# Merged attention weights computed inside the blocks ahead of them

## The reference

```python
def _L3_attn_ref ...
    k_eff = (W_dq.T @ W_uq.T @ W_uk).reshape(nh, hs, kvl)
    v_eff = (W_uv.T @ W_o.T).reshape(kvl, nh, hs).transpose(1, 0, 2)
    c_kv = x @ W_dkv.T
    q = (x @ W_dq.T @ W_uq.T).reshape(B, T, nh, hs).transpose(0, 2, 1, 3)
    q_lat = jnp.einsum('bhtd,hdl->bhtl', q, k_eff)
...
def _attention(x, Wq, Wkva, Wkvb, Wo):      # in _L3_ffn_ref
    q = (x @ Wq).reshape(b, t, H, D).transpose(0, 2, 1, 3)
    ckv = x @ Wkva
    kv_latent, k_rope = (ckv[:, :, :R], ckv[:, :, R:])
    kv = (kv_latent @ Wkvb).reshape(b, t, H, NOPE).transpose(0, 2, 1, 3)
...
    return y @ Wo
```

## Time and profile before

| | |
|---|---|
| median of 3 runs | 1993.07 us (1988.14 to 1995.74) |
| profiled execution, first to last instruction | 1991.5 us |
| instructions | 34855 |
| PE busy | 1615.1 us (81%) |
| DVE busy | 1231.2 us (62%) |
| ACT busy | 823.4 us (41%) |
| POOL busy | 606.1 us (30%) |
| mean granted TensorE clock | 0.892 of full speed |

### The profile page before, as it was taken

The page is one execution under the profiler, slowest core; times in us unless marked ns, Lnnn a source line. Parts: engine busy times, 40 slices in busy tenths (PEclk is TensorE's granted clock), DMA queues, the critical chain, the costliest instruction groups (busy, mean ns, idle before and its releaser), DMA issues. The chain is left out here.

```text
span 1991.5 us, 34855 instructions
## 1 busy us (share of the span) xinstructions
PE 1615.1 (81%) x12400; PEld 1077.5 (54%) x12400; DVE 1231.2 (62%) x4249; ACT 823.4 (41%) x1760; POOL 606.1 (30%) x742
## 2 busy tenths in 40 slices
PE   3378767888779897757988799978877888999888
PEld 1146434454547787644444366745546654677556
DVE  6868645575378999533666333326848875899632
ACT  2232345366227786732344443314643410333422
POOL 4605122430024535304531000022202115777221
PEclk8677877999879999878999898889988987999999
DMA  2000001320036777613321000022210000000000
GB/s 86 0 12 1 10 30 50 83 60 14 7 128 213 262 248 262 219 37 116 84 58 38 18 1 0 1 61 65 62 61 3 1 0 1 2 2 3 2 0 22
DMA packets 81332, 115.59 MB, mean 58 GB/s; under 512 B 8464, under 2 KB 62608, under 8 KB 80400
## 3 DMA queue, kind: packets, MB, share of 16 engines
q0 software_dynamic: 18432, 67.38, 9.7%
q1 hardware_dynamic: 60144, 44.90, 8.1%
q10 hardware_dynamic: 2592, 1.18, 0.3%
HBM read 88.85 MB, written 1.05 MB: 45 GB/s over the span
## 5 line engine op out<-in xcount | busy, mean ns | idle before, releaser
L2643 POOL DMA_INDIRECT f_rows<-tree_table,f_index x128 | 128.8, 1006 | 185.8 <-DVE f_index L2704 75.7
L2844 PE MATMUL f_ps_y<-f_rows,shared_sb 128*128 128x128 f32 x1024 | 129.2, 289 | 31.3 <-ACT f_rows L2916 31.3
L2916 ACT ACTIVATE f_rows<-f_rows,f_low_act 128x128 f32<-128x128 f32 x512 | 153.0, 387 | 0.8
L1667 ACT ACTIVATE x_probs<-x_ps_z 128x768 f32<-128x768 f32 (+1 forms) x128 | 117.4, 917 | 85.6 <-PE x_ps_z L1527 57.6
L82 POOL TENSOR_TENSOR rstd<-moments,shared_sb 128x12 f32<-128x12 f32 (+3 forms) x22 | 4.6, 207 | 480.9 <-DVE moments L66 480.8
L2844 PEld LDWEIGHTS f_ps_y<-f_rows,shared_sb 128*128 128x128 f32 x1024 | 124.5, 203 | 37.2 <-ACT f_rows L2916 33.9
L2743 DVE CUSTOM_DVE_ANT_0 f_rows<-f_rows,f_xn 128x128 f32<-128x128 f32 x512 | 111.3, 287 | 24.2 <-DMA f_rows<-tree_table,f_index 24.2
L1357 DVE TENSOR_REDUCE x_minus_max<-x_ps_s 128x4 f32<-128x1024 f32 x64 | 77.8, 1223 | 73.7 <-PE x_ps_s L1527 73.5
L2095 PE MATMUL f_ps_h<-f_xnT,weights 128*128 128x512 f32 x144 | 76.7, 661 | 2.4 <-ACT f_hT L2160 2.1
L2160 ACT ACTIVATE f_hT<-f_ps_h,weights 128x512 f32<-128x512 f32 x72 | 48.6, 685 | 71.4 <-PE f_ps_h L2095 69.7
L2072 DVE SCALAR_TENSOR_TENSOR x_tokens<-f_ps_y,f_chosen,x_tokens 128x128 f32 (+1 forms) x128 | 36.0, 344 | 67.1 <-PE f_ps_y L2107 67.1
(11 more groups left out here) (661 smaller groups left out, 4191.6 us busy)
## 6 DMA issues: line engine op xcount, KB each, us to landing
x_queries<-x_pieces SPq DMA_DIRECT2D x96, 64.0 KB, 2.1
x_keys<-x_pieces SPq DMA_DIRECT2D x84, 64.0 KB, 2.1
a_queries<-a_pieces SPq DMA_DIRECT2D x48, 64.0 KB, 2.1
weights<-w_L_ffn SPq DMA_DIRECT2D x1, 2953.5 KB, 9.9
a_keys<-a_pieces SPq DMA_DIRECT2D x42, 64.0 KB, 2.1
weights<-w_L_ffn SPq DMA_DIRECT2D x1, 2449.0 KB, 9.7
weights<-w_L_ffn SPq DMA_DIRECT2D x1, 2176.0 KB, 9.2
f_rows<-tree_table,f_index POOLq DMA_INDIRECT x128, 6.1
```

Source lines behind the costliest of these rows:

```text
L1667: a.activation(probs[:, r % HELD, :, :], ps_z[:, :, 0:WIDE], ACT.Exp, scale=scale).then_inc(exped, 1)
L2643: pool.indirect_dma_start(rows[:, place(u, j), tree, :], None, g.tree_table, bass.IndirectOffsetOnAxis(index[:, u % 2, low, j * TREES + tr ...
L2844: last = pe.matmul(ps_y[:, u % SUMS, j, :], g.ident, rows[:, place(u, j), tree, OUT + f * D:OUT + (f + 1) * D], start=False, stop=(low, j, ...
L2916: last = a.activation(row, row, ACT.Copy, scale=low_act[:, u % 3, j * TREES + tree, f:f + 1])
```

## The change

Two pieces of weight arithmetic move into the blocks ahead of the ones that use them.

1. The block with the latent attention's products goes. The seven products are issued by PE in the last turn of the experts, at e = 5, 6 and 7, between `up(e)` and `down(e - 1)`; the six copies by DVE after the additions of items 4, 5 and 6. The results lie in three tiles that now live for the whole program, the products in two further PSUM banks (the experts' block then uses all eight). The six semaphores move along, and so does their clearing, by SP, from one block to the next.
2. The rotary attention's eight product steps go from the start of `layer3_rotary` into slots 18 to 21 of `layer3_block`, in place of the 5 fillers of these slots: one group of line 3190 and one product of line 3197 in each, into the score bank that the MLP slots no longer use. DVE clears and copies its part in slot 18, after `add_mlp(17)`, and copies the products in slot 22. The 16 fillers and eight waits between the products go.

```diff
 def layer3_latent_attention(nc, g, w):
-        with ExitStack() as psums, nc.Block() as block:
...
+    weights = dict(w, **{n: m[:, :] for n, m in zip("qkv", g.latent_w)})
...
@@ layer2_experts, vector, turn @@
                     last.then_inc(added, 1)
+                    if is_last and e >= MERGED_AT - 1:
+                        take_merged(e)
...
+            def take_merged(e):
+                if e == MERGED_AT - 1:
+                    v.wait_ge(first_made, 1)
+                    v.tensor_copy(g.latent_w[0][:, :], ps_w[:, 0, 0:P])
+                    v.tensor_copy(wide[:, :], ps_w[:, 0, P:2 * P])
+                    v.tensor_copy(values[:, :], ps_w[0:32, 1, 0:P]).then_inc(first_ready, 1)
+                elif e == MERGED_AT:
+                    v.wait_ge(second_made, 1)
+                    v.tensor_copy(narrow[:, :], ps_w[0:32, 1, P:2 * P]).then_inc(second_ready, 1)
+                elif e == MERGED_AT + 1:
+                    v.wait_ge(third_made, 1)
+                    v.tensor_copy(g.latent_w[1][:, :], ps_w[:, 0, 0:P])
+                    v.tensor_copy(g.latent_w[2][:, :], ps_w[:, 0, P:2 * P]).then_inc(third_ready, 1)
+                    v.wait_ge(third_ready, 1)
...
@@ layer2_experts, tensor, turn @@
                             up(t, CH * e + c)
+                    if is_last and e >= MERGED_AT:
+                        merge(e)
...
+            def merge(e):
+                if e == MERGED_AT:
+                    pe.wait_ge(g.loaded["L3_attn"], 16)
+                    pe.matmul(ps_w[:, 0, 0:P], latent["dq"], latent["uqT"], start=True, stop=True)
+                    pe.matmul(ps_w[:, 0, P:2 * P], latent["uqT_plain"], latent["dq_wide"], start=True, stop=True)
+                    pe.matmul(ps_w[0:32, 1, 0:P], latent["uv"], latent["oT"], start=True, stop=True).then_inc(first_made, 1)
+                elif e == MERGED_AT + 1:
+                    pe.wait_ge(first_ready, 1)
+                    pe.matmul(ps_w[0:32, 1, P:2 * P], latent["uk"], wide[:, :], start=True, stop=True).then_inc(second_made, 1)
+                elif e == MERGED_AT + 2:
+                    pe.wait_ge(second_ready, 1)
+                    pe.matmul(ps_w[:, 0, 0:P], latent["dkv"], narrow[:, :], start=True, stop=True)
+                    pe.matmul(ps_w[:, 0, P:2 * P], latent["dkv"], values[:, :], start=True, stop=True).then_inc(third_made, 1)
...
@@ layer3_block, vector, end of a slot @@
+                if slot == MERGED_FROM:
+                    v.wait_ge(g.loaded["L3_ffn"], 16)
+                    v.memset(g.rotary_q[:, :, LATENTS:PLAIN], 0.0)
+                    v.tensor_copy(g.rotary_q[:, :, PLAIN:HEAD],
+                                  rotary["q"].rearrange("p (h d) -> p h d", h=HEADS)[:, :, PLAIN:HEAD])
+                if slot == MERGED_FROM + 4:
+                    v.wait_ge(parts_made, 8)
+                    v.tensor_copy(g.rotary_q[:, :, 0:LATENTS],
...
+                    v.tensor_copy(g.rotary_vo[:, :, :],
...
+                        .then_inc(parts_taken, 1)
+                    v.wait_ge(parts_taken, 1)
...
@@ layer3_block, tensor @@
+            def merge(j):
+                if j == 0:
+                    pe.wait_ge(g.loaded["L3_ffn"], 16)
+                    pe.wait_ge(max_ready, 2 * UNITS)
+                else:
+                    pe.wait_ge(parts_made, 2 * j)
+                for c in range(HEADS // 4):
...
+                last.then_inc(parts_made, 1)
...
...
-                fill_wait(pe, g, ps_c[:, :], 512, 5 if mlp_at(slot) is not None else 2)
+                if MERGED_FROM <= slot < MERGED_FROM + 4:
+                    merge(slot - MERGED_FROM)
+                else:
+                    fill_wait(pe, g, ps_c[:, :], 512, 5 if mlp_at(slot) is not None else 2)
...
@@ layer3_rotary, tensor @@
             pe.wait_ge(g.loaded["L3_ffn"], 16)
-            for j in range(4):
...
-                last.then_inc(w_made, 1)
-                fill_wait(pe, g, ps_s[:, 0, :], 512, 2)
-                pe.wait_ge(w_made, j + 1)
-            for c in range(4):
...
-                fill_wait(pe, g, ps_s[:, 0, :], 512, 2)
-                pe.wait_ge(w_made, 4 + c + 1)
             pe.wait_ge(const_ready, 1)
```

More of the change, by code:

```diff
@@ L2212, in layer3_block @@
                              "steps", "pool_steps", "const_ready"))
+        parts_made, parts_taken = sem("parts_made"), sem("parts_taken")
+        rotary = g.weights["L3_ffn"]
+        PLAIN, LATENTS, HEADS, HEAD = 32, 16, 16, 64
+        MERGED_FROM = ITEMS.index((MLP, 0)) + 2
         block = ctx.enter_context(nc.Block())
@@ L2481, in down @@
                 last.then_inc(y_made, 1)
+            def merge(j):
+                plain, both = (ps_s[:, i, :, :].rearrange("p j k -> p (j k)") for i in range(2))
+                rows = slice(PLAIN * j, PLAIN * (j + 1))
+                if j == 0:
[4 more added lines that the diff above has]
+                for c in range(HEADS // 4):
+                    h = 4 * c + j
+                    last = pe.matmul(plain[:, h * LATENTS:(h + 1) * LATENTS], rotary["q_plainT"][rows, c * P:(c + 1) * P],
+                                     rotary["kvbT"][rows, c * LATENTS:(c + 1) * LATENTS], start=True, stop=True)
+                last.then_inc(parts_made, 1)
+                rows = slice(HEAD * (j % 2), HEAD * (j % 2 + 1))
+                pe.matmul(both[rows, j // 2 * D:(j // 2 + 1) * D], rotary["kvb_blocks"][:, j * HEAD:(j + 1) * HEAD],
+                          rotary["o"][:, j * P:(j + 1) * P], start=True, stop=True).then_inc(parts_made, 1)
             transpose(0)
@@ L3079, in _ @@
             v.tensor_copy(halves16[:, :], w["halves"]).then_inc(const_ready, 1)
-            v.memset(w_q[:, :, LATENTS:PLAIN], 0.0)
-            v.tensor_copy(w_q[:, :, PLAIN:HD], w["q"].rearrange("p (h d) -> p h d", h=NH)[:, :, PLAIN:HD])
             def take_factor(part, of):
```

66 lines of the change are left out of this document (16 added, 50 removed).

## The result

| | before | changed |
|---|---|---|
| median of 5 runs each, taken together | 1988.52 us (1988.14 to 1995.74) | 1979.83 us (1976.32 to 1980.47) |
| ratio to before | | 0.9935, 95% interval 0.9917 to 0.9953 |
| span of the profiled execution | 1991.5 us | 1974.9 us |

The forecast was 1979.7 us. The medians lie 8.7 us apart, the means 12.1 us (1990.8 and 1978.7). Before's runs fall in two heaps, at 1988 and at 1993 to 1996, and the two medians caught different sides of them; by the ratio the gain is 0.65%, 12.9 us. The 13.4 us of the forecast are to be held against these, and not 1979.83 against 1979.7.

The account below looks back on a forecast made before the run. No engine bounds the whole kernel; two seams between blocks are on the path. Gains of 3.4 and 13.1 less 0.7 and 2.4 make 13.4 us, so 1993.07 becomes 1979.7 us; the stated range is 1973.5 to 1988.

Parts of the forecast that it names:

- The seam of the latent attention: Between experts and latent attention: the latent products' block goes, 5.8 us gained, nothing behind it becomes late.
- Products among the experts: Experts' last turn: 14 product records at 0.146 us cost 2.0 us, plus a 0.35 us PE wait at e = 6.
- Part 1: Latent products moved into the experts' last turn: 5.8 - 2.0 - 0.35 = 3.4 us gained (1.4 to 4.1).
- Rotary start: Start of the rotary attention: ACT's first copy 13.65 us earlier, 0.5 lost to the late clock rise; 13.1 us gained.
- 3 x 0.24: MLP slots 19 to 21: products busy 2.58 us against the fillers' 2.34 at 1.2 GHz; 0.7 us lost.
- 2 x 1.21: MLP slots 22 and 23: the clock stays down, 6.31 us each instead of 5.10; 2.4 us lost.
- A third term: MLP slot 18: DVE's memset and copy, 0.6 us, come at the slot's end and cost nothing.
- The cover of 0.95 us: MLP slots: DVE idles 0.95 us for POOL, which hides its memset and copies; without that cover 1.5 us.
- The first rival: MLP slots: the clock returns in slot 21 or 22 as before, giving 2.4 us back; 1977.3 us, chance 0.25.
- The cold start: Rotary attention: clock at 1.2 GHz from fillers to first scores; 6.5 us gained, 1986.6 us, chance 0.12.
- dip: Experts' last turn: clock falls to 0.50; 10 us long gives 1984.7 us, chance 0.10; without end 1998.0, chance 0.04.
- The first tokens: Rotary attention: its first tokens would wait for something else, so almost no gain; 1992.8 us, chance 0.04.

Follow-up runs that it names:

- early: Changed kernel with DVE's first three copies of the latent products ahead of item 4's additions instead of behind them; 1974.31 us (one run).
- twice: Changed kernel with each of the six latent products issued twice into the same place; 1980.70 us (one run).
- part1: Kernel before with only the latent products moved into the experts' last turn, rotary products left in place; 1986.97 us, ratio to before 0.9982.
- both: The changed kernel run once more, unaltered, against the kernel before on the same chip; 1976.95 us, ratio to before 0.9937.
- part2: Kernel before with only the rotary products moved into the MLP slots, latent products keeping their block; 1983.09 us, ratio to before 0.9967.
- slot17: Changed kernel with the rotary products one slot earlier, in slots 17 to 20; 1976.09 us, ratio to before 0.9928.
- best: Changed kernel with five fillers kept behind the products, as in fills, and the copies moved, as in early; 1973.12 us, ratio to before 0.9908.
- fills: Changed kernel with the five fillers kept behind the rotary products in slots 18 to 21; 1972.76 us (one run).
- nofill: Changed kernel without the fillers (3 a slot) ahead of the rotary attention's first slot of scores; 1978.49 us, ratio to before 0.9928.
- gap: part1 with the five fillers of slots 18 to 21 taken out and nothing put in their place; 1988.80 us, ratio to before 0.9981.
- hot: Changed kernel with 10 fillers in slots 16 to 18, 3 behind the products in slots 19 to 21, 8 in 22 and 23; 1985.50 us (one run).
- fills5: Five further runs of the same kernel as fills, against the kernel before; 1974.16 us, ratio to before 0.9904.

## Why the prediction was right

That the median meets the forecast to 0.1 us is luck. The forecast stands on 1993.07, the median of three runs of the kernel before; five runs put it at 1988.52. What was right is the gain: 13.4 us forecast, 12.5 in the profiled pair and 12.9 by the ratio, with errors inside its terms that in part cancel.

**The seam of the latent attention: right.** 5.8 us worked out, 5.81 measured, and nothing became late behind it: the latent attention's first scores come 24.4 us after the block's start, where they came after 24.8. SP's further clearing cost nothing that the trace shows.

**Products among the experts: the sum right by luck.** 2.0 for the records and 0.35 for the wait were 2.35; measured 2.4. But the 2.0 is 14 x 0.146, and there are six products and 12 records, which give 1.75 and a sum of 2.1. `early` puts the wait at 0.15, `twice` the 12 records at 1.66; what was left out is the other 0.6, about 0.3 us for each of the two groups that stand alone. The two records too many and the wait that was too long made up for it. Part 1 comes to 5.8 - 2.4 = 3.4 us, as worked out; part 1 alone measured 3.6.

**Rotary start: right within 0.4 us.** 13.65 us to ACT's copy, measured 13.56. The clock rose later than estimated: at 0.50 up to 1652.6, 4.6 us behind the first filler and not 4, so the chain behind the copy took 0.8 us more, not 0.5. This term is not one number: the chain takes 6.9 to 7.0 us in `both`, `part2`, `slot17`, `early` and `best`, where the clock is up by the time of ACT's copy, 7.5 in `fills` and 7.7 here, where it comes 1.0 and 1.4 us behind it, and 8.2 in `twice`, at 2.4 us. That the step is sized rightly doesn't show that the fillers help: `nofill` is as fast up to the first scores without them.

**The MLP slots: 3.6 us where 3.1 were worked out, and both terms mis-sized.** The term "3 x 0.24" came from busy times, 2.58 against 2.34. Measured, a slot at 1.2 GHz with products takes 6.91 us against 6.31, so 0.6 more. By their starts, from the first filler to the next `down` it is 2.14 us (1623.71 to 1625.85), from the group to the next `down` 2.44 (1609.93 to 1612.37), and the transpose ahead and the first step of `down` behind take 0.3 more together. The weight load of that `down` starts 0.43 us ahead of it behind the fillers, and with it behind the products (the row at 1612.36). The kernel before:

```profile
1625.42 0.76 PEld L2479 LDWEIGHTS x_ps_z<-weights,x_hT 128*128 128x128 f32 x2 [0.28 <-issue]
1625.85 0.64 PE L2479 MATMUL x_ps_z<-weights,x_hT 128*128 128x128 f32 x2
```

The cost shows in the intervals of slots 20, 21 and 22, so 1.8 instead of 0.7. In slot 19 it is nothing: the 6.31 us of the prediction are one interval, that of slot 21; before the change slot 19 took 5.10 and slot 20 5.67. The term "2 x 1.21" was too large: the low stretch lasted one slot longer and not two (27.3 us against 17.1, less what lies in slot 18), and it ended in the fillers of slot 22; 1.2, and 0.3 more where the fall comes earlier in its slot. A third term was put at nothing and cost 0.33: in slot 18 DVE's memset and copy of 128x512 stand beside POOL's first step of the reciprocal deviation, which takes 0.52 us there and 0.20 elsewhere, and DVE's layer norm waits for POOL. It takes 0.52 in all eleven kernels that have the two instructions there and 0.20 in the three that don't (before, `part1`, `gap`); which of the two does it was not separated. The cover of 0.95 us that the prediction named was a wait for just the instruction that they slow. The Trainium skill, "SBUF — State Buffer", "Who interferes with whom", says that VectorE and GpSimd share one port pair with an exclusive lock, which VectorE's copies can take in their two-port modes; the row agrees in direction, with 0.3 us, and can't say who held the pair.

**The clock.** That the products would not bring it up was right: 25.78 of 26.00 us busy at 0.50 in the changed kernel, 30.20 of 30.20 in `part2`. The reason given was thinner than it had to be: it spoke of the products, but in `gap` the clock stays down 23.9 us without them, and `fills` shows that they do no harm where the fillers stay. The Trainium skill, "TensorE: Matmul & The Clock Gate", Part 1, has sustained activity release the clock. By a simple reading of that rule, busy is enough; these stretches with a fully busy PE at 1.2 GHz speak against it. The first rival, the clock that returns in slot 21 or 22, came half: it returned in slot 22, in the fillers that stand there again, but so late that this slot took 6.90 us; slot 23, which the forecast had at the low clock as well, took 5.10.

**The other rivals.** The cold start came in its mechanism, 5 us at 0.50, but at the price of 0.8 us; cold all through and without the fillers (`nofill`) the start costs nothing up to the first scores. A start that is cold all through with the fillers in place was not seen; the dearest was `twice`, with 1.3 us. No dip came in the experts: in the changed kernel it stands at 1.00 from 1296 to 1309.6, and `twice`, with double the products, has no low stretch there either. The first tokens waited for nothing else.

Taken together 3.4 + 12.75 - 3.6 = 12.55 us against the forecast's 13.4.

## What to carry to other kernels

Small weight products belong into a dense TensorE stream of an earlier part: they cost 0.11 to 0.16 us a record and about 0.3 us a group, where a block of their own costs the whole chain of handovers. But where they take the place of fillers, keep the fillers behind them and look at the granted clock: the products alone kept the engine busy for 26 us and more without bringing it back, and with the fillers kept it was low for 7 us in three traces of three. It is no rule: five fillers a slot without products left it low for 17. Price a replaced piece by intervals of the slot at the clock that will hold there, not by busy times, and look which other engine the covered copy slows.

## What the runs showed of the hardware

- TensorE can be busy without a pause for 30 us and stay at 1.2 GHz (`part2`, 30.20 of 30.20 us: f32 products with 128 and 256 columns, one-row bias products, 16-column products, and in the last two slots five fillers each); in another kernel it fell from 2.4 GHz while busy 5.00 of every 5.00 us (`hot`). With five fillers of 128x512 bf16 behind the products of each slot it was back after 3.4 us, twice (`fills`); with as many and no products it stayed low for 17.1 us (before).
- An f32 group of eight records with 16 columns takes 1.06 us at 2.4 GHz and 1.89 at 1.2 (line 2514).
- A low clock need not cost anything: without fillers and products the MLP part took 40.1 us with 23.9 us at 0.50, and 41.9 us before the change with 17.1.
- A VectorE memset of 128x256 and copy of 128x512 f32, 0.55 us together, lengthen a GpSimd step of 0.20 us beside them to 0.52, in eleven kernels of eleven.
- Two times (1 - mean granted clock) times the span gives the time at 1.2 GHz of a run for which there is no trace: 395 us in `fills5` against 428 before.
